# Turned first product with a copied stationary matrix, three results on the way and a load table in an adaLN block with a mixture of experts

## The chip, the cores and the metric

The kernel runs on one core of one Trainium2 chip. The metric is the device time of one execution in microseconds. PE is TensorE (its weight loads stand as PEld), DVE is VectorE, ACT is ScalarE, POOL is GpSimd, SP is SyncE, which issues most of the DMAs. A q behind an engine's name (POOLq, SPq) is its sequencer, which runs register and semaphore instructions itself.

## The reference

An input x of 16 positions x 256 rows x 256 features becomes a diffusion and reaction term, which then goes through one transformer block with a mixture of experts. Cut to what matters:

```python
x_in = diffuse(x, zX, zY, zR)                       # 16 x 256 rows of 256 features
attn = causal_attention(layernorm(x_in) @ in_proj)  # 16 heads over the 16 positions
x1   = x_in + attn @ out_proj
hn2  = layernorm(x1).reshape(4096, 256)
gates = top-2 of softmax(hn2 @ router_w.T)          # 8 experts
hmid = gelu(hn2 @ w1[e])                            # 256 -> 512, for each chosen expert e
y    = (hmid * gate) @ w2[e]                        # 512 -> 256
out  = x + x1 + y                                   # y summed over the two experts of a row
```

## The kernel before, in words

**Two halves.** A loop over `g` (32 groups of 128 rows, with a few steps ahead and behind) does diffusion, norms, attention and routing: DVE multiplies and sums the attention, PE projects and turns. Rows that are routed are scattered by POOL into a buffer in DRAM, sorted by expert (`scatter`, two indirect DMAs for each group). After each of seven sets of groups DVE makes a table of tiles of 128 rows of one expert (`route_tiles`): 71 tiles in all, with the expert in `tab`, the buffer row in `tabr`, and a count in `tabw`.

**A tile's steps.** SP loads a tile (`tile_in`). PE turns it (`turn_in`, L1062, into `b_x`), ACT applies the norm's weights while it copies it to `xT` (L565). PE multiplies by the first matrix (`up`, L1071): `xT` is the stationary operand, the expert's 512 columns of `w1_s`, addressed by a register, are the moving one, and the result `b_h` is 128 rows x 512. ACT applies the Gelu (L590) into `hm`; PE turns `hm` with four transposes (`turn_h`, L1078) into `b_t`, ACT copies that to `hmT` (L594), and PE multiplies by the second matrix (`down`, L1086, into `b_y`). ACT (L604, tiles below 47) or DVE (L764, tiles from 47 on) scales the result into one of five buffers `y`. POOL adds it to the output in DRAM with an indirect DMA that accumulates (`add_y`, L492).

**The order of the tiles.** A list written out by hand (`SLOTS`) places 39 first steps of tiles inside the loop; the other tiles follow behind the attention, one slot for each tile (`LEFT`). A slot (a, b, c, d) turns tile a in, multiplies tile b up, tile c down, and gives tile d out. In the first slot of `LEFT` a is 39 and d is 36.

**The order of the adds.** Two tiles of different experts may hold the same row, and then the second add must not start before the first has landed. Up to tile 36 POOL simply waits for the add before. From tile 37 on, `add_y` reads a threshold from the table `tabw` into a register (L485): it is one step lower where the tile's rows follow those of the tile before in the same expert's part of the buffer. POOL then waits for the semaphore against that register; a tiny instruction on `passed` (L487, "the check" below) carries the wait. Whatever the table says, at most two adds are on the way, with a semaphore for each parity. Adds 38 to 42 alternate with the scatters of the last five groups (L457).

```python
if j > IN_LOOP:
    behind = pool.value_load(tabw[0:1, j:j + 1], min_val=16, max_val=16 * ALL)
    pool.wait_ge(y_added[(j - 1) % 2], behind)
    pool.tensor_tensor(passed[:, j - IN_LOOP:j - IN_LOOP + 1], power[:, 0:1], power[:, 0:1], ALU.add)
elif j >= 1:
    pool.wait_ge(*added_to(j - 1))
if j >= 2:
    pool.wait_ge(*added_to(j - 2))
```

**The bulk loads.** SP loads w1 (eight loads of 512 KB, at g = 1 to 8), w2 (eight, at g = 3 to 10) and three of the four copies of x to the output (1 MB each, at g = 1, 3, 5) between the loads of the loop.

Of the kernel before, what the change touches and what calls it, by code (L numbers as in the profile page):

```python
# [5 lines left out]
P = 128  # L6
# [11 lines left out]
def adaln_moe_block(nc, x, zX, zY, zR, ln1_w, ln1_b, in_w, in_b, out_w, out_b, ln2_w, ln2_b,  # L18
# [25 lines left out]
    CAP = G * P + 2 * P  # L44
    ROW = H + 1 + E
    RING = 10
    NX = 4
    NY = 5
    NM = 12
# [7 lines left out]
    with ctx:  # L57
# [9 lines left out]
        def pair(name):  # L67
# [62 lines left out]
        tab = sb("tab", [P, ALL], I32)  # L130
        iota_i = tab[:, 0:TMAX + 3 * E + 1]
        tabr = sb("tabr", [P, ALL], I32)
        tabw_1 = sb("tabw_1", [P, 2 * (ALL // 2 + 1)], I32)
        tabw = tabw_1[:, 1:ALL + 1]
        passed = sb("passed", [P, 44])
        apart = tt[:, 1, 0:(TMAX + E - 1) // E, :].rearrange("p a b -> p (a b)").bitcast(I32)
        live = sb("live", [P, TMAX])

# [14 lines left out]
            sums_ready scaled du_ready stats1 stats2 rstd xhat1 xhat2 hT_ready hT_sb h2T_ready h2T_sb  # L153
            qkv_ready qk_sb v_sb sc_ready exp_ready pv_piece pv_used aT_sb o_ready x1_ready lg_ready lg_sb
            rt_sub rt_exp rt_m rt_cum rt_cum_sb slots_ready tab_ready pre_ready
            x_tr xT_sb h_ready gelu_done hT2_ready hmT_sb y_ready y_sb pre_done
            dve_chain pool_chain""".split()
        s = {n: sem(n) for n in names}
        x_in, y_added = pair("x_in"), pair("y_added")
        x1_added = [sem(f"x1_added{i}") for i in range(4)]  # L160
        xin_in = [sem(f"xin_in{i}") for i in range(NX)]
        scattered = [sem(f"scattered{i}") for i in range(NG)]
# [59 lines left out]
        for g in range(G + 3):  # L222
            for n in PLACES[WANT[g]]:
                step = next_slot((g, n))
                SLOTS[g, n].append(step)
                turned, raised, lowered, given = [i + (j is not None) for i, j in zip((turned, raised, lowered, given), step)]
        IN_LOOP = given
        while given < ALL:
            step = next_slot((G + 3, 0))
            LEFT.append(step)  # L230
            turned, raised, lowered, given = [i + (j is not None) for i, j in zip((turned, raised, lowered, given), step)]
# [8 lines left out]
        COUNT_FIRST = 10  # L240
        BY_DVE = FEW
        IDLE_UNTIL = min(g for g, n in SLOTS if any(b is not None for a, b, c, d in SLOTS[g, n]))
        W1_FROM = 1
        W2_FROM = 3

        def runs(g0, n):

# [10 lines left out]

        def added_to(j):

            return y_added[j % 2], 16 * (j // 2 + 1)

        def half_of(g):
            return ORDER[g]
# [13 lines left out]
        def _(sp):  # L278
# [44 lines left out]
            sp.wait_ge(s["bias_split"], 2)  # L323
            sp.dma_start(bias[1:2, :].bitcast(F32), blo.bitcast(F32)).then_inc(s["bias_lo_in"], 16)

            def tile_in(j):

                if j in FIRST:
                    r = group_of(j)
                    sp.wait_ge(s["tab_ready"], r + 1)  # L330
                    sp.wait_ge(scattered[r], 32 * len(GROUPS[r]))
                if j == TAIL:
                    sp.wait_ge(s["pre_done"], 16 * E)
                if j >= NX:
                    sp.wait_ge(s["x_tr"], j - NX + 1)
                if j >= NM:
                    sp.wait_ge(*added_to(j - NM))
                row = sp.value_load(tabr[0:1, j:j + 1], min_val=0, max_val=E * CAP - P)
# [11 lines left out]
            for g in range(-AHEAD, G + 3):  # L350
                if 3 <= g + AHEAD + 1 < G:
                    load(g + AHEAD + 1)
                if 0 <= g - W1_FROM < E:
                    e = g - W1_FROM
                    sp.dma_start(w1_s[:, e * HC * F:(e + 1) * HC * F].rearrange("p (k f) -> p k f", k=HC),
                                 w1[e].rearrange("(k p) f -> p k f", p=P)).then_inc(s["w1_in"], 16)
                if 0 <= g - W2_FROM < E:
                    e = g - W2_FROM
                    sp.dma_start(w2_s[:, e * FC * H:(e + 1) * FC * H].rearrange("p (k h) -> p k h", k=FC),
                                 w2[e].rearrange("(k p) h -> p k h", p=P)).then_inc(s["w2_in"], 16)  # L360
                if g % 2 and 1 <= (g + 1) // 2 < NCOPY:
                    copy_x((g + 1) // 2)
# [11 lines left out]
            for j in (ALL - 2, ALL - 1):  # L374
                sp.wait_ge(*added_to(j))

        @block.gpsimd
        def _(pool):
# [18 lines left out]
            def later_constants():  # L397
                link(pool.memset(ones_b[:, :], 1.0))

                pool.affine_select(out=lower[:, :], in_=ones_b[:, :], compare_op=ALU.is_gt, fill=0.0, base=0,  # L400
                                   pattern=[[1, P]], channel_multiplier=-1).then_inc(s["const_ready"], 1)
                pool.memset(ones_r[:, :].bitcast(F32), 1.0).then_inc(s["const_ready"], 1)
                links_of = [pool.iota(iota_i[:, 0:TMAX], [[1, TMAX]], base=0, channel_multiplier=0),
                            pool.iota(iota_i[:, TMAX:TMAX + E], [[CAP, E]], base=P, channel_multiplier=0),
                            pool.iota(iota_i[:, TMAX + E:TMAX + 2 * E], [[CAP, E]], base=P - 1, channel_multiplier=-1),
                            pool.iota(iota_i[:, TMAX + 2 * E:TMAX + 3 * E], [[P, E]], base=E * CAP, channel_multiplier=1),
                            pool.iota(iota_i[:, TMAX + 3 * E:TMAX + 3 * E + 1], [[1, 1]], base=0, channel_multiplier=1),
                            *[pool.iota(idt[:, g:g + n], [[B, n]], base=p * B + c * P, channel_multiplier=1)
                              for g, c, p, n in ((0, 0, 0, FEW), (FEW, 1, 0, FEW), (2 * FEW, 0, FEW, S - FEW), (AGAIN, 1, FEW, S - FEW))]]
                links_of.append(pool.iota(tabw_1[:, :].rearrange("p (a b) -> p a b", b=2), [[16, ALL // 2 + 1], [0, 2]],  # L410
                                          base=0, channel_multiplier=0))
                link(links_of[-1])
                pool.tensor_copy(iota_f[:, :], iota_i[:, :]).then_inc(s["const_ready"], 1)
# [64 lines left out]
            def add_y(j):  # L478

                pool.wait_ge(s["y_sb"], j + 1)  # L480
                if j in FIRST:
                    for i in range(4):
                        pool.wait_ge(x1_added[i], 16 * len([g for g in range(ENDS[group_of(j)]) if g % 4 == i]))
                if j > IN_LOOP:
                    behind = pool.value_load(tabw[0:1, j:j + 1], min_val=16, max_val=16 * ALL)  # L485
                    pool.wait_ge(y_added[(j - 1) % 2], behind)
                    pool.tensor_tensor(passed[:, j - IN_LOOP:j - IN_LOOP + 1], power[:, 0:1], power[:, 0:1], ALU.add)  # L487
                elif j >= 1:
                    pool.wait_ge(*added_to(j - 1))
                if j >= 2:  # L490
                    pool.wait_ge(*added_to(j - 2))
                pool.indirect_dma_start(out_rows, bass.IndirectOffsetOnAxis(ap=tags[:, j % NM, 0:1].bitcast(U32), axis=0),  # L492
                                        y[:, j % NY, :], None, compute_op=ALU.add).then_inc(y_added[j % 2], 16)

            def scatter_at(g, n):
                for step in SCATTER.get((g, n), ()):
# [34 lines left out]
        def _(act):  # L531
# [55 lines left out]

            def gelu(j):
                act.wait_ge(s["h_ready"], j + 1)
                act.activation(hm[:, :], b_h[:, :], ACT.Gelu).then_inc(s["gelu_done"], 1)  # L590

            def turned_h(j):
                act.wait_ge(s["hT2_ready"], j + 1)
# [11 lines left out]
                               scale=tags[:, j % NM, bass.ds(e + 1, 1)]).then_inc(s["y_sb"], 1)  # L605

            def slot(a, b, c, d):
                if c is not None:
                    turned_h(c)
                if d is not None and d < TAIL:  # L610
                    result(d)
# [85 lines left out]
                    place(g, n)  # L697
            slot(*LEFT[0])
            odds(NG - 1)
            for a, b, c, d in LEFT[1:]:  # L700
                slot(a, b, c, d)

        @block.vector
        def _(dve):
# [144 lines left out]
            def route_tiles(r):  # L849
# [43 lines left out]
                else:  # L893
# [4 lines left out]
                    need(step)  # L898
                    step = tick(dve.tensor_scalar(apart[:, 0:m], apart[:, 0:m], P, -16, ALU.is_equal, ALU.mult))
                    need(step)  # L900
                    dve.tensor_tensor(tabw[:, a:b], apart[:, 0:m], tabw[:, a:b], ALU.add).then_inc(s["tab_ready"], 1)

            for g in range(-AHEAD, G + 3):
                T = ORDER[g][1] + 1 if 0 <= g < G else 0
# [137 lines left out]
        def _(pe):  # L1042
# [32 lines left out]
            def turn_h(j):  # L1075
# [2 lines left out]
                    mm = pe.transpose(b_t[:, k * P:(k + 1) * P], hm[:, k * P:(k + 1) * P], ident[:, :])  # L1078
                mm.then_inc(s["hT2_ready"], 1)

            def down(j, e):
                pe.wait_ge(s["hmT_sb"], j + 1)
                if j >= 1:
                    pe.wait_ge(s["y_sb"], j)
                for k in range(FC):
# [9 lines left out]
            loaded = {}  # L1095

            def slot(a, b, c):
                if a == 0:
                    pe.wait_ge(s["w1_in"], 16 * E)
                    pe.wait_ge(s["w2_in"], 16 * E)  # L1100
                if b is not None:
                    loaded[b] = next_expert(b)
                if c is not None:
                    turn_h(c)
                if b is not None:
                    up(b, loaded[b])
                if a is not None:
# [174 lines left out]
```

## Time and profile before

| | |
|---|---|
| median of 3 runs | 658.73 us (656.2 to 659.06) |
| profiled execution, own time | 656.47 us |
| its span in the trace | 654.4 us |
| outside the span | 2.07 us |
| mean granted clock of TensorE | 0.955 |
| PE busy | 591.0 us (90%) |
| DVE, ACT, POOL busy | 437.4 us, 375.5 us, 428.5 us |

Matmuls are pipelined and their ends are modelled, so a matmul's own duration is longer than the distance from one to the next; where a pace matters it is read from starts. A tile's steps are spread over the engines, so the stage behind the attention (from about 507 us on) is read by the distance of the same step from tile to tile.

### The profile page before, as it was taken

To read this page: it belongs to the slowest core of one execution; us is meant where nothing else is said; L and a number is where in the kernel's file an instruction comes from. 1 tells how busy PE (TensorE), PEld (TensorE's weight loads), DVE (VectorE), ACT (ScalarE), POOL (GpSimd) and SP (SyncE) were. 2 spreads that over 40 slices of the span, in tenths; PEclk is the share of its full clock that TensorE was granted. 3 is DMA by queue.
4 is the path that set the end of the run, shared out by engine and by line. 5 is a ranking of instruction groups with operands and counts; after the bars stand their busy time and mean duration, and the time that the engine had idled before them with its cause. 6 is when DMAs were issued, how large, how long until landed. Compare 5 with 4: busy or idle time off the path is not lost.

```text
span 654.4 us, 10903 instructions
## 1 busy us (share of the span) xinstructions
PE 591.0 (90%) x2842; PEld 420.0 (64%) x2842; DVE 437.4 (67%) x1012; ACT 375.5 (57%) x860; POOL 428.5 (65%) x516
## 2 busy tenths in 40 slices
PE   6599988788969989999999999999698999999991
PEld 6356656566746757766666777777475666666661
DVE  4576899779996999999977999969950500111110
ACT  2443553357646776768887876665355655444440
POOL 4576785865894488597898788834784774444442
PEclk9887998879889999999999999999998999999997
DMA  7386662441342224334344333532344545444422
GB/s 204 100 303 187 200 195 72 116 91 49 75 99 50 58 74 83 74 59 81 83 107 76 73 67 66 108 50 43 82 78 57 103 87 90 67 66 67 67 33 24
DMA packets 61775, 59.89 MB, mean 92 GB/s; under 512 B 17610, under 2 KB 57299, under 8 KB 61652
## 3 DMA queue, kind: packets, MB, share of 16 engines
q0 software_dynamic: 18288, 23.28, 21.9%
q1 hardware_dynamic: 43428, 35.91, 19.5%
q8 instruction: 26, 0.43, 0.3%
q14 instruction: 33, 0.27, 0.1%
HBM read 35.89 MB, written 27.46 MB: 97 GB/s over the span
## 4 chain that ended last, share of the span: by engine, by line
PE 51%; DVE 19%; POOL 12%; issue 6%; ACT 5%; DMA 4%; SPq 1%; POOLq 0%; ACTq 0%; DVEq 0%
PE b_h L1071 13%; PE b_y L1086 13%; PE b_at L1251 5%; DVE qk_prod L938 5%; PE b_qk L1189 4%; DVE sc L946 4%; POOL xs_d L457 3%; PE b_t L1078 3%; PE b_at L1179 3%; DVE pv_prod L1015 3%; DMA out_dram<-y,tags 2%; PE b_v L1189 2%; POOL out_dram L492 2%; PE b_x L1062 2%; POOL dev L443 1%
## 5 line engine op out<-in xcount | busy, mean ns | idle before, releaser
L492 POOL DMA_INDIRECT out_dram<-y,tags x71 | 124.2, 1750 | 30.1 <-issue 24.3
L1086 PE MATMUL b_y<-w_s,hm_hmT 128*128 x568 | 135.2, 381 | 4.9 <-ACT y L604 3.3
L1071 PE MATMUL b_h<-w_s,xT 128*128 x284 | 134.7, 597 | 0.3
L1086 PEld LDWEIGHTS b_y<-w_s,hm_hmT 128*128 128x128 f32 x568 | 102.4, 190 | 19.2 <-issue 8.2
L938 DVE TENSOR_TENSOR qk_prod<-q,kv 128x1024 f32<-128x1024 f32 (+2 forms) x80 | 91.3, 1165 | 2.4 <-ACT kv L630 1.4
L1015 DVE TENSOR_TENSOR pv_prod<-kv,pr 128x1024 f32<-128x1024 f32 (+2 forms) x80 | 85.5, 1113 | 6.8 <-PE b_at L1251 5.6
L764 DVE TENSOR_SCALAR y<-b_y,tags,live 128x256 f32<-128x256 f32 x24 | 13.0, 544 | 113.0 <-PE b_y L1086 113.0
L1251 PE MATMUL b_at<-ident,pv_prod 128*128 128x128 f32 x544 | 72.4, 288 | 13.2 <-DVE pv_prod L1015 13.1
L457 POOL DMA_INDIRECT xs_d<-ring,slot_row x64 | 70.7, 1105 | 18.9 <-issue 18.1
L946 DVE TENSOR_REDUCE sc<-qk_prod 128x64 f32<-128x1024 f32 (+2 forms) x80 | 82.1, 1051 | 0.3
L1251 PEld LDWEIGHTS b_at<-ident,pv_prod 128*128 128x128 f32 x544 | 65.1, 149 | 18.3 <-issue 15.2
L1071 PEld LDWEIGHTS b_h<-w_s,xT 128*128 128x128 f32 x284 | 48.9, 192 | 35.3 <-issue 35.1
L590 ACT ACTIVATE hm_hmT<-b_h 128x512 f32<-128x512 f32 x71 | 42.5, 598 | 45.6 <-PE b_h L1071 45.6
L1189 PE MATMUL b_qk<-wqkv,hT 128*128 128x512 f32 x128 | 67.2, 650 | 0.3 <-ACT hT L565 0.3
L594 ACT ACTIVATE hm_hmT<-b_t 128x512 f32<-128x512 f32 x71 | 42.6, 600 | 36.0 <-PE b_t L1078 36.0
L565 ACT ACTIVATE xT<-b_x,ln 128x128 f32<-128x128 f32 x142 | 57.0, 458 | 3.6 <-PE b_x L1062 3.6
L442 POOL TENSOR_SCALAR dev<-mv 128x2 f32<-128x2 f32 (+1 forms) x37 | 14.8, 401 | 65.6 <-DVE mv L995 56.5
L1062 PEld LDWEIGHTS b_x<-ident,xin 128*128 128x128 f32 x142 | 19.8, 141 | 41.3 <-issue 39.1
L487 POOL TENSOR_TENSOR passed<-power 128x1 f32<-128x1 f32 x34 | 7.4, 218 | 58.6 <-DMA out_dram<-y,tags 54.6
L1078 PE MATMUL b_t<-ident,hm_hmT 128*128 128x128 f32 x284 | 43.4, 276 | 0.3 <-ACT hm_hmT L590 0.2
L629 ACT ACTIVATE q<-b_qk 128x256 f32<-128x256 f32 x32 | 12.0, 376 | 51.3 <-PE b_v L1189 51.3
L430 POOL TENSOR_TENSOR du<-du,xp 128x256 f32<-128x256 f32 x28 | 27.5, 981 | 20.1 <-ACT xud L545 19.9
(186 smaller groups left out, 1085.2 us busy)
## 6 DMA issues: line engine op xcount, KB each, us to landing
xin<-xs_d SPq DMA_DIRECT2D x71, 128.0 KB, 2.1
w_s<-in_L_ffn_w_dram SPq DMA_DIRECT2D x16, 512.0 KB, 4.5
xp<-in_x_dram SPq DMA_DIRECT2D x32, 128.0 KB
xud<-in_x_dram SPq DMA_DIRECT2D x32, 128.0 KB
out_dram<-x POOLq DMA_DIRECT2D x32, 128.0 KB, 3.2
xud<-in_x_dram SPq DMA_DIRECT2D x32, 126.0 KB
tags<-xs_d SPq DMA_DIRECT2D x71, 4.5 KB, 2.0
out_dram<-y,tags POOLq DMA_INDIRECT x71, 3.9
```

Of the source, the lines that this page charges most:

```text
L457: pool.indirect_dma_start(xs_d, bass.IndirectOffsetOnAxis(ap=slot_row[:, k, g:g + 1], axis=0), ring[:, g % RING, :], None).then_inc(scatte ...
L492: pool.indirect_dma_start(out_rows, bass.IndirectOffsetOnAxis(ap=tags[:, j % NM, 0:1].bitcast(U32), axis=0), y[:, j % NY, :], None, comput ...
L565: ins = act.activation(dst[:, c * P:(c + 1) * P], bank[:, c * P:(c + 1) * P], ACT.Identity, scale=ln[:, 2 * k, c:c + 1], bias=ln[:, 2 * k ...
L594: act.activation(hmT[:, :], b_t[:, :], ACT.Copy).then_inc(s["hmT_sb"], 1)
L938: made.append(tick(dve.tensor_tensor(qk_prod[:, m % 2, 0:(t1 - t0) * H].rearrange("p (t h) -> p t h", h=H), q[:, g % 2, :].rearrange("p (o ...
L946: summed.append(tick(dve.tensor_reduce(scv.rearrange("p n t -> p t n")[:, t0:t1, :], qk_prod[:, m % 2, 0:(t1 - t0) * H].rearrange("p (t n ...
L1015: dve.tensor_tensor(pv_prod[:, at % NPV, 0:(t1 - t0) * H].rearrange("p (t n d) -> p t n d", n=NH, d=D), kv[:, values_at(v, t0):values_at(v ...
L1071: mm = pe.matmul(b_h[:, :], xT[:, k * P:(k + 1) * P], w1_s[:, bass.ds(e * (HC * F) + k * F, F)], start=(k == 0), stop=(k == HC - 1))
L1078: mm = pe.transpose(b_t[:, k * P:(k + 1) * P], hm[:, k * P:(k + 1) * P], ident[:, :])
L1086: mm = pe.matmul(b_y[:, 0:H], hmT[:, k * P:(k + 1) * P], w2_s[:, bass.ds(e * (FC * H) + k * H, H)], start=(k == 0), stop=(k == FC - 1))
L1189: mm = pe.matmul(bank[:, 0:b - a], hT[:, k, :], wqkv[:, k, a:b], start=False, stop=(k == HC - 1))
L1251: mm = pe.matmul(b_at[:, k * P:(k + 1) * P], pv_prod[:, at % NPV, lo:lo + P], ident[:, :], start=(m == 0 and t == 0 and k == 0), stop=(m = ...
```

## The change

From tile 39 on (`TURNED`), the first product comes out turned: the matrix w1 of the tile's expert is the stationary operand and `xT` the moving one, so that no transposes and no copy of them follow. The stationary operand needs a fixed place, so ACT reads the tile's expert from the table and copies the 1024 columns of the matrix into one of five buffers that the attention's products have left free (`matrix`, two tiles ahead). `b_h` and `b_t` alternate as the product's bank. Three adds may be on the way in place of two (`NA`): there are two tables of thresholds, and `add_y` reads and waits for both, one behind the other. The bulk loads follow a table (`BULK`), and PE waits for w1 before the first `up` and for w2 before the first `down`.

```diff
+    NA = 3
...
-        tabw_1 = sb("tabw_1", [P, 2 * (ALL // 2 + 1)], I32)
-        tabw = tabw_1[:, 1:ALL + 1]
-        passed = sb("passed", [P, 44])
+        behind_all = sb("behind_all", [P, NA - 1, NA * (ALL // NA + 2)], I32)
+        behind = [behind_all[:, k, NA - 1 - k:NA - 1 - k + ALL] for k in range(NA - 1)]
+        passed = sb("passed", [P, (NA - 1) * 44])
...
-        W1_FROM = 1
-        W2_FROM = 3
+        BULK = {0: ("a0",), 1: ("a1",), 2: ("a2",), 3: ("a3",), 4: ("a4",), 5: ("a5",), 6: ("a6", "x1"), 7: ("a7", "b0"),
+                8: ("b1", "b2"), 9: ("b3", "b4"), 10: ("b5", "b6"), 11: ("b7", "x2"), 13: ("x3",)}
...
+        w1_bufs = [qk_prod[:, 0, :], qk_prod[:, 1, :]] + [pv_prod[:, i, :] for i in range(NPV)]
+        NW = len(w1_bufs)
+        def w1_buf(j):
+            return w1_bufs[(j - TURNED) % NW]
+        def hidden(j):
+            return ((b_h, hm), (b_t, hmT))[(j - TURNED) % 2]
...
                 if j > IN_LOOP:
-                    behind = pool.value_load(tabw[0:1, j:j + 1], min_val=16, max_val=16 * ALL)
-                    pool.wait_ge(y_added[(j - 1) % 2], behind)
-                    pool.tensor_tensor(passed[:, j - IN_LOOP:j - IN_LOOP + 1], power[:, 0:1], power[:, 0:1], ALU.add)
+                    for k in range(1, NA):
+                        least = pool.value_load(behind[k - 1][0:1, j:j + 1], min_val=16, max_val=16 * ALL)
+                        pool.wait_ge(y_added[(j - k) % NA], least)
+                        at = (NA - 1) * (j - IN_LOOP) - k
+                        pool.tensor_tensor(passed[:, at:at + 1], power[:, 0:1], power[:, 0:1], ALU.add)
                 elif j >= 1:
                     pool.wait_ge(*added_to(j - 1))
-                if j >= 2:
-                    pool.wait_ge(*added_to(j - 2))
+                if j >= NA:
+                    pool.wait_ge(*added_to(j - NA))
...
+            def matrix(j):
+                if j == TURNED:
+                    act.wait_ge(s["sc_ready"], G)
+                    act.wait_ge(s["pv_used"], PIECES[G])
+                if j in FIRST:
+                    act.wait_ge(s["tab_ready"], group_of(j) + 1)
+                e = act.value_load(tab[0:1, j:j + 1], min_val=0, max_val=E - 1)
+                if j - TURNED >= NW:
+                    act.wait_ge(s["h_ready"], j - NW + 1)
+                act.activation(w1_buf(j), w1_s[:, bass.ds(e * (HC * F), HC * F)], ACT.Copy).then_inc(s["w1_made"], 1)
...
             odds(NG - 1)
+            for j in (TURNED, TURNED + 1):
+                matrix(j)
             for a, b, c, d in LEFT[1:]:
                 slot(a, b, c, d)
+                if a is not None and a + 1 < ALL:
+                    matrix(a + 1)
...
-                    dve.tensor_tensor(tabw[:, a:b], apart[:, 0:m], tabw[:, a:b], ALU.add).then_inc(s["tab_ready"], 1)
+                    for k in range(NA - 1):
+                        ins = dve.tensor_tensor(behind[k][:, a:b], apart[:, 0:m], behind[k][:, a:b], ALU.add)
+                    ins.then_inc(s["tab_ready"], 1)
...
+            def up_turned(j):
+                bank, _ = hidden(j)
+                pe.wait_ge(s["w1_made"], j - TURNED + 1)
+                pe.wait_ge(s["xT_sb"], j + 1)
+                pe.wait_ge(s["gelu_done"], j - 1)
+                if j == TURNED + 1:
+                    pe.wait_ge(s["hmT_sb"], TURNED)
+                w = w1_buf(j).rearrange("p (k f) -> p k f", k=HC)
+                for i in range(FC):
+                    for k in range(HC):
+                        mm = pe.matmul(bank[:, i * P:(i + 1) * P], w[:, k, i * P:(i + 1) * P], xT[:, k * P:(k + 1) * P],
+                                       start=(k == 0), stop=(k == HC - 1))
+                mm.then_inc(s["h_ready"], 1)
...
-                if a == 0:
+                if b == 0:
                     pe.wait_ge(s["w1_in"], 16 * E)
+                if c == 0:
                     pe.wait_ge(s["w2_in"], 16 * E)
```

## Rows read from the trace of the kernel before

**Rows 1.** Chain that ended last, one tile's steps: start, length in us, engine and line
```profile
553.21 1.72 PE b_h L1071 x4
554.93 0.22 PE b_x L1062 x2
555.14 1.73 PE b_y L1086 x8
556.87 0.44 PE b_t L1078 x4
557.31 1.72 PE b_h L1071 x4
```

**Rows 2.** The same chain at its end, 623 us on
```profile
623.26 0.34 POOLq L485
...
623.92 0.19 POOL passed L487
624.12 0.46 issue
...
632.85 3.70 DMA out_dram<-y,tags
636.55 0.07 issue
636.62 0.19 POOL passed L487
```

**Rows 3.** POOL's waits, 538 to 650 us: total us, times, longest
```profile
POOL passed L487 <- DMA out_dram<-y,tags: 50.6, 21, 3.0
POOL passed L487 <- DVE y L764: 3.8, 4, 1.4
```

**Rows 4.** POOL's timeline: start, length, instruction, idle before and its releaser
```profile
510.71 1.54 POOL L492 DMA_INDIRECT out_dram<-y,tags  x1 [0.68 <-issue]
...
528.97 1.61 POOL L492 DMA_INDIRECT out_dram<-y,tags  x1 [0.16 <-issue]
...
533.53 1.62 POOL L492 DMA_INDIRECT out_dram<-y,tags  x1 [0.17 <-issue]
...
537.84 1.58 POOL L492 DMA_INDIRECT out_dram<-y,tags  x1 [0.22 <-ACT y L604]
...
539.80 1.57 POOL L492 DMA_INDIRECT out_dram<-y,tags  x1 [0.16 <-issue]
...
645.09 0.19 POOL L487 TENSOR_TENSOR passed<-power 128x1 f32<-128x1 f32 x1 [2.33 <-DMA out_dram<-y,tags]
645.43 1.57 POOL L492 DMA_INDIRECT out_dram<-y,tags  x1 [0.15 <-issue]
```

**Rows 5.** Lines L57 (block's end), L485 (ns min/median/max, starts), L492 (538 to 650)
```profile
L57 POOLq DRAIN  x1: 9095/9095/9095, 645.0 to 645.0; - x1
...
L485 POOLq TENSOR_LOAD <-tabw x34: 283/292/632, 509.0 to 642.6; - x34
...
DMA to landing us min/median/max: 3.7/3.9/4.5
```

**Rows 6.** ACT's timeline as the attention ends, and line L572
```profile
507.68 0.24 ACT L639 ACTIVATE odd<-odd 128x40 f32<-128x40 f32 x1
507.82 0.58 ACT L594 ACTIVATE hm_hmT<-b_t 128x512 f32<-128x512 f32 x1
...
L572 ACT ACTIVATE bias<-kv x1: 1056/1056/1056, 6.9 to 6.9; 1x1024 fp32r<-1x1024 f32 x1
```

**Rows 7.** ACT's timeline over one tile
```profile
563.17 0.60 ACT L590 ACTIVATE hm_hmT<-b_h 128x512 f32<-128x512 f32 x1 [1.12 <-PE b_h L1071]
```

**Rows 8.** Chain that ended last: 32 turns of the attention's products
```profile
483.71 3.56 PE b_at L1251 x32
```

**Rows 9.** Stages: us, busy us (count) of PE, PEld, DVE, ACT, POOL, clock, DMA share, GB/s
```profile
45.00:130.00 85.00, 74.05 (x380) 53.94 (x378) 69.72 (x188) 38.33 (x112) 63.29 (x87) 0.92 0.55 168
...
507.00:640.00 133.00, 132.21 (x588) 91.29 (x585) 20.72 (x67) 67.22 (x140) 67.46 (x75) 1.00 0.45 72
```

More of the change, by code:

```diff
@@ L155, in adaln_moe_block @@
             rt_sub rt_exp rt_m rt_cum rt_cum_sb slots_ready tab_ready pre_ready
-            x_tr xT_sb h_ready gelu_done hT2_ready hmT_sb y_ready y_sb pre_done
+            x_tr xT_sb h_ready gelu_done hT2_ready hmT_sb w1_made y_ready y_sb pre_done
             dve_chain pool_chain""".split()
         s = {n: sem(n) for n in names}
-        x_in, y_added = pair("x_in"), pair("y_added")
+        x_in = pair("x_in")
+        y_added = [sem(f"y_added{i}") for i in range(NA)]
         x1_added = [sem(f"x1_added{i}") for i in range(4)]
@@ L227, in adaln_moe_block @@
         IN_LOOP = given
+        TURNED = turned
         while given < ALL:
@@ L259, in added_to @@
         def added_to(j):
-            return y_added[j % 2], 16 * (j // 2 + 1)
+            return y_added[j % NA], 16 * (j // NA + 1)
+        w1_bufs = [qk_prod[:, 0, :], qk_prod[:, 1, :]] + [pv_prod[:, i, :] for i in range(NPV)]
[4 more added lines that the diff above has]
+            return ((b_h, hm), (b_t, hmT))[(j - TURNED) % 2]
         def half_of(g):
@@ L324, in _, with bulk @@
             sp.dma_start(bias[1:2, :].bitcast(F32), blo.bitcast(F32)).then_inc(s["bias_lo_in"], 16)
+            def bulk(what, i):
+                if what == "a":
+                    sp.dma_start(w1_s[:, i * HC * F:(i + 1) * HC * F].rearrange("p (k f) -> p k f", k=HC),
+                                 w1[i].rearrange("(k p) f -> p k f", p=P)).then_inc(s["w1_in"], 16)
+                elif what == "b":
+                    sp.dma_start(w2_s[:, i * FC * H:(i + 1) * FC * H].rearrange("p (k h) -> p k h", k=FC),
+                                 w2[i].rearrange("(k p) h -> p k h", p=P)).then_inc(s["w2_in"], 16)
+                else:
+                    copy_x(i)
             def tile_in(j):
@@ L352, in _ @@
                     load(g + AHEAD + 1)
[L353 to L362, printed above, removed]
+                for what in BULK.get(g, ()):
+                    bulk(what[0], int(what[1]))
                 for n in range(NPLACES):
@@ L373, in _ @@
                 sp.wait_ge(x1_added[i], 16 * (G // 4))
-            for j in (ALL - 2, ALL - 1):
+            for j in range(ALL - NA, ALL):
                 sp.wait_ge(*added_to(j))
@@ L409, in later_constants @@
                               for g, c, p, n in ((0, 0, 0, FEW), (FEW, 1, 0, FEW), (2 * FEW, 0, FEW, S - FEW), (AGAIN, 1, FEW, S - FEW))]]
-                links_of.append(pool.iota(tabw_1[:, :].rearrange("p (a b) -> p a b", b=2), [[16, ALL // 2 + 1], [0, 2]],
+                links_of.append(pool.iota(behind_all[:, :, :].rearrange("p k (a b) -> p k a b", b=NA), [[0, NA - 1], [16, ALL // NA + 2], [0, NA]],
                                           base=0, channel_multiplier=0))
@@ L484, in add_y @@
                 if j > IN_LOOP:
-                    behind = pool.value_load(tabw[0:1, j:j + 1], min_val=16, max_val=16 * ALL)
-                    pool.wait_ge(y_added[(j - 1) % 2], behind)
-                    pool.tensor_tensor(passed[:, j - IN_LOOP:j - IN_LOOP + 1], power[:, 0:1], power[:, 0:1], ALU.add)
+                    for k in range(1, NA):
[3 more added lines that the diff above has]
+                        pool.tensor_tensor(passed[:, at:at + 1], power[:, 0:1], power[:, 0:1], ALU.add)
                 elif j >= 1:
                     pool.wait_ge(*added_to(j - 1))
-                if j >= 2:
-                    pool.wait_ge(*added_to(j - 2))
+                if j >= NA:
+                    pool.wait_ge(*added_to(j - NA))
                 pool.indirect_dma_start(out_rows, bass.IndirectOffsetOnAxis(ap=tags[:, j % NM, 0:1].bitcast(U32), axis=0),
-                                        y[:, j % NY, :], None, compute_op=ALU.add).then_inc(y_added[j % 2], 16)
+                                        y[:, j % NY, :], None, compute_op=ALU.add).then_inc(y_added[j % NA], 16)
             def scatter_at(g, n):
@@ L589, in gelu @@
                 act.wait_ge(s["h_ready"], j + 1)
-                act.activation(hm[:, :], b_h[:, :], ACT.Gelu).then_inc(s["gelu_done"], 1)
+                if j < TURNED:
+                    act.activation(hm[:, :], b_h[:, :], ACT.Gelu).then_inc(s["gelu_done"], 1)
+                else:
+                    bank, dst = hidden(j)
+                    act.wait_ge(s["y_ready"], j - 1)
+                    act.activation(dst, bank[:, :], ACT.Gelu).then_inc(s["gelu_done"], 1)
+            def matrix(j):
[8 more added lines that the diff above has]
+                act.activation(w1_buf(j), w1_s[:, bass.ds(e * (HC * F), HC * F)], ACT.Copy).then_inc(s["w1_made"], 1)
             def turned_h(j):
@@ L607, in slot @@
             def slot(a, b, c, d):
-                if c is not None:
+                if c is not None and c < TURNED:
                     turned_h(c)
@@ L1079, in turn_h @@
                 mm.then_inc(s["hT2_ready"], 1)
-            def down(j, e):
-                pe.wait_ge(s["hmT_sb"], j + 1)
+            def up_turned(j):
[11 more added lines that the diff above has]
+                mm.then_inc(s["h_ready"], 1)
+            def down(j, e):
+                hmT = hidden(j)[1] if j >= TURNED else hm_hmT[:, F:2 * F]
+                if j < TURNED:
+                    pe.wait_ge(s["hmT_sb"], j + 1)
+                else:
+                    pe.wait_ge(s["gelu_done"], j + 1)
                 if j >= 1:
@@ L1102, in slot @@
                     loaded[b] = next_expert(b)
-                if c is not None:
+                if c is not None and c < TURNED:
                     turn_h(c)
-                if b is not None:
+                if b is not None and b < TURNED:
                     up(b, loaded[b])
+                if b is not None and b >= TURNED:
+                    up_turned(b)
                 if a is not None:
```

## The prediction

> **What bounds the kernel now.** I read the stages first, then the chain that ended last, then POOL's waits. Behind the attention PE is busy without a break (132.21 of 133 us at full clock) and a tile takes 557.31 - 553.21 = 4.10 us: 1.72 up, 0.22 turning the next tile in, 1.73 down, 0.44 for four transposes [rows 1, 9]. But near 623 us the chain leaves PE and goes from add to add through the DMAs [rows 2]. In the 27 checks from add 44 to add 70 POOL waited 21 times for an add to land (50.6 us) and 4 times for a result [rows 3]. The add is therefore a second chain that runs almost as slowly as PE, so I price both.
>
> One link of it: an add's DMA lands 3.70 us after its start, the semaphore takes 0.07, the check 0.19, and the next add starts 0.15 behind it [rows 2, 4]: 4.1 us at best. The median to landing from 538 us on is 3.9 [rows 5]; with the 0.07 that is 4.0 to the next check, so I take 4.0 + 0.34 = 4.34. Two adds of which the second need not wait start 539.80 - 537.84 = 1.96 apart [rows 4]. How many must wait? Working the routing out from the inputs, 20 of the tiles 44 to 70 do not continue the rows of the tile before (the 21st wait of the row, at 628 us, coincides with a result), and 7 do. The chain before could thus do 20 x 4.34 + 7 x 1.96 = 100.5 us; the row says 645.43 - 537.84 = 107.6, PE's pace gives 27 x 4.10 = 110.7 less the lag that add 43 had. The adds have only some 7 us to spare.
>
> **TensorE's gain.** Transposes go: 0.44. The turned product has eight 128-column products, each as two passes as in L1071's four records for two: 16 passes with a new stationary matrix each. Not in the trace with these operands; the nearest row is 32 transposes with 32 new stationary matrices and 128 moving columns in 3.56 us, 0.111 each [rows 8], so 16 x 0.111 = 1.78 against 1.72. A tile becomes 1.78 + 0.22 + 1.73 = 3.73 us, 0.37 less; for 32 tiles 11.8 us of PE work. It counts only if the adds keep up.
>
> **ScalarE.** The copy of 1024 columns took 1.06 us on one partition [rows 6]; I take that for 128, since 512 columns of 128 partitions take 0.60 [rows 7] and doubling that bounds it at 1.20. ACT loses the copy of the turned hidden values (0.60, same size as rows 7) and had 1.12 us idle before each Gelu [rows 7] beside as much before the other: hidden, tile for tile. At the entry it is not: two matrices are copied between the exponentials (507.68) and the older copy of tile 38 (507.82), behind a table read of about 0.5. That puts result 37, and add 37, some 0.5 + 2 x 1.06 = 2.6 us later.
>
> **The adds: what the change adds.** Each add now reads two thresholds, and the second read stands behind the first check. From read to check is 623.92 - 623.26 = 0.66, of which the read was 0.34 against a median of 0.29, so 0.61 [rows 2, 5]. Behind a check that had just been reached by a read the add starts 0.19 + 0.46 = 0.65 later, not 0.34 [rows 2]. Does the second read run while the first check still waits? A sequencer instruction that follows a waiting check is to be seen once: the block's end, on POOLq, starts at 645.0, although the engine stood idle for 2.33 us before, and the check of the last add is released at 645.09 [rows 4, 5]. So I take it that the read waits. From release to add: about 0.58 to the second check (the read starts 0.04 ahead of the check's own start), 0.65 to the add: 1.23 in place of 0.34, 0.9 more for each add that waits. The bounds: 0.2 (the read is hidden, a check of 0.19 remains), 0.58 (the read counts, the longer way to the add does not), 1.25 (the slowest read, 0.63 [rows 5]).
>
> The Trainium skill, page "Perfetto Trace Analysis", section "GPSIMD Engine Instruction", draws it otherwise: an instruction for the engine is pushed into a wait queue, and the sequencer is then ready for the next one. By that rule the second read would run under the first wait and the sum would be 658, the first rival below; the start of the block's end [rows 5] is this trace's evidence against it.
>
> Third place on the way: it helps only where two tiles in a row need not wait, which of 27 is one place (65, 66), at most some 2 us, and waits for an add that landed long ago elsewhere. Nothing.
>
> **The sum, against the profiled execution's 656.47 us.**
> 1. Add 37 started at 510.71 [rows 4]; entry 2.6 and its second read 0.9: 514.2.
> 2. Adds 38 to 43. A round of two scatters, check and add takes 533.53 - 528.97 = 4.56 on POOL alone [rows 4], 4.78 with the second check. Two of the six follow their predecessor's rows: 2 x 4.78; four wait: 4 x (4.34 + 0.9 = 5.24). 30.5, so add 43 starts at 544.7, 6.9 later than its 537.84.
> 3. Adds 44 to 70: 20 x 5.24 + 7 x 2.16 = 119.9, 12.3 more than 107.6. PE needs 27 x 3.73 = 100.7 there; it waits for the five y buffers and its gain is lost.
> 4. From the last add's start to the end: as before.
>
> 656.5 + 6.9 + 12.3 = 675.7; I say **675**. The last scatters land a few us later, and with them tile 47's load; its result is wanted only some ten us after. The median of the runs before stands 2.3 us above the profiled execution, which is less than anything at issue.
>
> **Costed at nothing.** Bulk loads by a table: in 45 to 130 us DMAs are busy 0.55 of the time [rows 9], and the waits view of that stretch names no DMA, so neither earlier w1 nor later copies of x shorten a wait; the last w2 load moves next to the first tile's load, which has ten us before the first down. Without that cover, 2 us either way. One more DVE instruction in six table makings: below 0.3 each, up to 1.6 if DVE is on the path every time. PE's waits for the weights: met long before.
>
> **Rivals.**
> - *The second read is hidden under the first check's wait* (not slower). The extra is 0.2: add 37 +2.8; rounds 6 x 4.78 = 28.7 (+1.6); then 20 x 4.54 + 7 x 2.0 = 104.8 (-2.8). 656.5 + 2.8 + 1.6 - 2.8 = about 658, no change. It decides at an extra of 0.2 to 0.3 for each waiting add; against it stands the start of the block's end. 0.13.
> - *The adds keep up and PE's gain comes out* (faster). The entry is hidden too and a landing link stays at 4.34: 100.7 in place of 107.6, about 650. Against it: the table read is in the chain of waits itself [rows 2]. 0.06.
> - *Stationary loads do not hide behind products of 128 columns.* If load and product add up, a pass costs 0.22, the turned product 3.56 and a tile 5.51: 32 x 1.4 = 45 us more than before, about 700. Against it: the 32 turns at 0.111 [rows 8], each with a load of the same size. 0.05. The Trainium skill's page "TensorE: Matmul & The Clock Gate", section "Part 3: Packing small matmuls — row/col tiling", says that a load overlaps products in flight only where the row group differs, which is this rival; the turns of rows 8 use the full array and disagree.
> - *The adds' chain sets the end, as summed.* 0.76. With 0.58 extra: entry and rounds +5.3, then 20 x 4.92 + 7 x 2.16 = 113.5 (+5.9): 667.7. With 1.25: about 684.
>
> **Range and chances.** 657 to 684: the main case by its bounds and the upper half of the first rival; main case alone 667 to 684. Less than 0.5% (3 us, about what a measurement of this kernel can tell from no change) faster or slower comes from the first rival: 0.11; faster: the second and a little of the first, 0.08; slower 0.81.
>
> **What would show it.** Right: between the two checks of one add some 0.6 us with a table read in it and 0.65 to the add; adds that wait 5.2 us apart; PE with gaps, its tile 3.7 us where it runs free, turned products at 0.11 us a pass; ACT idle between copies; the chain that ended last made of adds from about 515 us. Wrong: second reads that end before the first check starts; adds 4.3 apart; PE without gaps to the end; or passes at 0.2 us.

## The result and the profile after

The changed kernel takes 671.64 us (median of 6 runs, 666.78 to 677.12) where the kernel before, run beside it, takes 656.38 us (6 runs, 651.08 to 659.06). The ratio is 1.0235, with a 95% interval of 1.019 to 1.0281: slower by 15.3 us. The forecast was 675. The profiled execution of the changed kernel took 673.18 us itself, with a span of 671.0.

The page first: the span, PE's busy time, PE's and its clock's slices, then the two rows of the adds (the check L506 and the add's DMA L511).

```profile
span 671.0 us, 11687 instructions
...
PE 585.6 (87%) x3098; PEld 444.1 (66%) x3098; DVE 437.3 (65%) x1018; ACT 385.8 (57%) x860; POOL 434.5 (65%) x550
...
PE   5698998698879989999999999997889969999920
...
PEclk9887977989869999999999999999889979999965
...
L511 POOL DMA_INDIRECT out_dram<-y,tags x71 | 123.5, 1739 | 37.4 <-issue 32.1
...
L506 POOL TENSOR_TENSOR passed<-power 128x1 f32<-128x1 f32 x68 | 16.8, 314 | 62.4 <-DMA out_dram<-y,tags 49.9
```

PE has less to do than before and ends earlier: in the last two slices it is busy 2 tenths and not at all. The granted clock falls to 6 and 5 tenths in these slices; in the one before both stand at 9 (full speed is 2.4 GHz, the lower level 1.2). POOL's checks stand idle 49.9 us for adds to land, 68 of them now, two for each add.

The stages, in the columns of [rows 9]:

```profile
507.00:640.00 133.00, 123.64 (x835) 114.78 (x833) 20.54 (x67) 77.29 (x140) 66.12 (x98) 0.97 0.41 68
640.00:671.00 31.00, 2.68 (x8) 1.73 (x8) 1.09 (x2) 0.00 (x0) 10.65 (x16) 0.55 0.25 29
```

In the last 31 us PE works 2.68 us and ACT not at all; what is left is POOL's adds. The whole loss arises behind add 36, the last before the entry (the stretch in which the attention ends and the first two matrices are copied): this add starts at 506.07 where it started at 506.54 before. From POOL's timelines, first the kernel before, then adds 36, 37 and 43 of the changed one:

```profile
506.54 1.54 POOL L492 DMA_INDIRECT out_dram<-y,tags  x1 [3.00 <-issue]
```

```profile
506.07 1.54 POOL L511 DMA_INDIRECT out_dram<-y,tags  x1 [2.84 <-issue]
...
512.83 1.54 POOL L511 DMA_INDIRECT out_dram<-y,tags  x1 [0.69 <-issue]
...
543.16 1.58 POOL L511 DMA_INDIRECT out_dram<-y,tags  x1 [0.82 <-issue]
```

PE's timeline over one turned tile (start, length, line, operation, tiles, count):

```profile
516.96 1.95 PE L1134 MATMUL b_h<-xT,pv_prod 128*128 128x128 f32 x16
518.75 0.38 PE L1104 MATMUL b_x<-ident,xin 128*128 128x128 f32 x2
518.96 1.89 PE L1147 MATMUL b_y<-w_s,hm_hmT 128*128 x8
520.69 1.95 PE L1134 MATMUL b_t<-xT,pv_prod 128*128 128x128 f32 x16
```

By starts, as in [rows 1]: the turned product with its 16 passes takes 518.75 - 516.96 = 1.79 us, and a tile 520.69 - 516.96 = 3.73, where it took 4.10. TensorE's part of the change does what it says.

POOL's timeline near the end, one add behind the other (L506 is a check, L511 the add's DMA):

```profile
645.57 0.19 POOL L506 TENSOR_TENSOR passed<-power 128x1 f32<-128x1 f32 x1 [2.54 <-DMA out_dram<-y,tags]
646.13 0.19 POOL L506 TENSOR_TENSOR passed<-power 128x1 f32<-128x1 f32 x1 [0.38 <-issue]
646.79 1.56 POOL L511 DMA_INDIRECT out_dram<-y,tags  x1 [0.46 <-issue]
650.67 0.19 POOL L506 TENSOR_TENSOR passed<-power 128x1 f32<-128x1 f32 x1 [2.32 <-DMA out_dram<-y,tags]
...
662.09 1.56 POOL L511 DMA_INDIRECT out_dram<-y,tags  x1 [0.46 <-issue]
```

In the kernel before an add that had waited started 0.34 us behind the start of its only check [rows 4]. Here it takes 646.79 - 645.57 = 1.22: 0.56 to the second check and 0.66 to the add. The chain that ended last shows what fills the 0.56 (start, length, what; POOLq is POOL's own sequencer):

```profile
643.03 2.50 issue
645.53 0.23 POOLq L503
...
645.85 0.15 POOLq L503
...
646.13 0.19 POOL passed L506
646.33 0.25 issue
```

L503 is the second read of a threshold. It starts at 645.53, 0.04 us before the first check, after 2.50 us in which nothing ran. It did not run under the wait. Where the first wait was met already it is otherwise; add 66, in the same view:

```profile
639.61 0.35 POOLq L503
...
640.38 0.63 POOL passed L506
```

Here the second read starts 0.77 us ahead of the first check, while POOL still works on add 65; in the seven such adds from 44 on it is 0.62 to 0.78. So it is the wait not yet met that holds the read back here, and not a busy engine.

Last, POOL's, DVE's and PE's waits from 510 to 660 us (total us, times, longest); POOL's and DVE's lines read the same from 544 to 662 us, the stretch of adds 44 to 70:

```profile
POOL passed L506 <- DMA out_dram<-y,tags: 47.7, 20, 2.7
...
DVE y L804 <- DMA out_dram<-y,tags: 21.1, 5, 4.7
...
PE b_x L1104 <- DMA tags<-xs_d: 5.1, 1, 5.1
```

From add 44 on twenty checks wait for a landing, the number that the routing gave. The second line is new: DVE waits for a free `y` buffer, which the late adds still hold.

### The profile page after: what moved, and what is told of

Its sections match the earlier page's. It is cut to its first block and busy times, and to the rows that moved or that the text cites. A ratio compares the mean times of both kernels' runs of the same rounds, so it can differ in the third digit from the quotient of the medians.

```text
span 671.0 us, 11687 instructions
## 1 busy us (share of the span) xinstructions
PE 585.6 (87%) x3098; PEld 444.1 (66%) x3098; DVE 437.3 (65%) x1018; ACT 385.8 (57%) x860; POOL 434.5 (65%) x550
## 5 line engine op out<-in xcount | busy, mean ns | idle before, releaser
L511 POOL DMA_INDIRECT out_dram<-y,tags x71 | 123.5, 1739 | 37.4 <-issue 32.1
L1147 PE MATMUL b_y<-w_s,hm_hmT 128*128 x568 | 138.0, 387 | 8.9 <-DVE y L804 4.2
L1315 PE MATMUL b_at<-ident,pv_prod 128*128 128x128 f32 x544 | 74.0, 292 | 10.5 <-DVE pv_prod L1057 10.3
L1315 PEld LDWEIGHTS b_at<-ident,pv_prod 128*128 128x128 f32 x544 | 67.0, 152 | 15.3 <-issue 12.3
L1113 PE MATMUL b_h<-w_s,xT 128*128 x156 | 75.0, 604 | 0.3
L1253 PE MATMUL b_qk<-wqkv,hT 128*128 128x512 f32 x128 | 69.7, 672 | 0.0
L506 POOL TENSOR_TENSOR passed<-power 128x1 f32<-128x1 f32 x68 | 16.8, 314 | 62.4 <-DMA out_dram<-y,tags 49.9
L1253 PEld LDWEIGHTS b_qk<-wqkv,hT 128*128 128x128 f32 x128 | 25.8, 213 | 22.5 <-issue 20.2
L1113 PEld LDWEIGHTS b_h<-w_s,xT 128*128 128x128 f32 x156 | 27.3, 194 | 20.0 <-issue 19.9
L1243 PE MATMUL b_at<-wo,aT 128*128 128x256 f32 x128 | 39.0, 430 | 0.0
L1104 PE MATMUL b_x<-ident,xin 128*128 128x128 f32 x142 | 28.0, 280 | 11.0 <-DMA tags<-xs_d 11.0
```

The source lines that it names most:

```text
L1104: mm = pe.transpose(b_x[:, k * P:(k + 1) * P], xin[:, i, k * P:(k + 1) * P], ident[:, :])
L1113: mm = pe.matmul(b_h[:, :], xT[:, k * P:(k + 1) * P], w1_s[:, bass.ds(e * (HC * F) + k * F, F)], start=(k == 0), stop=(k == HC - 1))
L1147: mm = pe.matmul(b_y[:, 0:H], hmT[:, k * P:(k + 1) * P], w2_s[:, bass.ds(e * (FC * H) + k * H, H)], start=(k == 0), stop=(k == FC - 1))
L1243: mm = pe.matmul(b_at[:, H:2 * H], aT[:, k, :], wo[:, k, :], start=False, stop=(k == HC - 1))
L1253: mm = pe.matmul(bank[:, 0:b - a], hT[:, k, :], wqkv[:, k, a:b], start=False, stop=(k == HC - 1))
L1315: mm = pe.matmul(b_at[:, k * P:(k + 1) * P], pv_prod[:, at % NPV, lo:lo + P], ident[:, :], start=(m == 0 and t == 0 and k == 0), stop=(m = ...
```

## Experiments

The theory is the prediction's: an add that waits carries a second read and a longer way to its DMA, and this chain sets the end. The rivals are another source of the loss (ScalarE's copies, the turned product, the load table) and a cause in the number of adds on the way instead of the read. One stretch settles most of it without the run-to-run shift of the attention: from the start of add 36 to the start of add 70, read from POOL's timeline of each run. Before, it is 645.43 - 506.54 = 138.9 us. The run with the load table alone, whose program behind add 36 is that of the kernel before, gives 139.8: differences of 1 us in this stretch tell nothing. The expected times were reckoned from some 656 us for the kernel before; beside the experiments it took 652.93 and 652.52, so it is the ratios that compare.

| kernel | add 36 to add 70, us | against before | ratio of medians (95%) |
|---|---|---|---|
| changed kernel | 156.0 | +17.1 | 1.0235 (1.019 to 1.0281) |
| two adds on the way | 134.95 | -3.94 | 0.9916 (0.9877 to 0.9956) |
| three adds alone | 156.7 | +17.8 | 1.0307 (1.0263 to 1.035) |
| both reads first | 141.1 | +2.2 | 1.0029 (0.9992 to 1.0065) |
| third read | 172.1 | +33.2 | one run: 689.01 us |
| two adds, earlier copies | 132.8 | -6.1 | 0.992 (0.9886 to 0.9953) |
| load table alone | 139.8 | +0.9 | 1.000 (0.9964 to 1.0036) |

**Two adds on the way.** The changed kernel with one number back:

```diff
-    NA = 3
+    NA = 2
```

> The changed kernel with two adds on the way and one threshold read for each add, as before; the turned product, the matrix copies and the load table stay. If the second read behind the first check is the cost, an add that waits costs 4.34 us again in place of 5.24; the copies at the entry still put add 37 about 1.5 us later (as the trace after shows); the 27 last adds take 100.5 to 104 us, because TensorE now delivers a tile every 3.73 us: about 651 us, faster than before. Rival, the turned product or its copies on ScalarE are the cost: near 670 us, as after. Rival, the load table is the cost: also near 670.

It took 648.11 us (10 runs, 644.64 to 652.41) beside 652.93 of the kernel before: 0.8% faster than that one (0.4 to 1.2%), and far below the changed kernel. Its POOL timeline at the end:

```profile
631.19 0.19 POOL L506 TENSOR_TENSOR passed<-power 128x1 f32<-128x1 f32 x1 [2.26 <-DMA out_dram<-y,tags]
631.53 1.56 POOL L511 DMA_INDIRECT out_dram<-y,tags  x1 [0.15 <-DVE y L804]
635.46 0.19 POOL L506 TENSOR_TENSOR passed<-power 128x1 f32<-128x1 f32 x1 [2.36 <-DMA out_dram<-y,tags]
635.79 1.57 POOL L511 DMA_INDIRECT out_dram<-y,tags  x1 [0.15 <-issue]
```

With one read and one check the way from release to add is 0.34 again, and two waiting adds stand 635.79 - 631.53 = 4.26 us apart. So ScalarE's copies, the turned product and the load table together give more than they cost.

**Three adds alone.** The kernel before with only the adds' part of the change (`NA`, two tables of thresholds, the loop of reads and checks, the DVE instruction that fills the second table):

```diff
+    NA = 3
...
-                    behind = pool.value_load(tabw[0:1, j:j + 1], min_val=16, max_val=16 * ALL)
-                    pool.wait_ge(y_added[(j - 1) % 2], behind)
+                    for k in range(1, NA):
+                        least = pool.value_load(behind[k - 1][0:1, j:j + 1], min_val=16, max_val=16 * ALL)
+                        pool.wait_ge(y_added[(j - k) % NA], least)
...
```

> The kernel before with nothing changed but the adds: three on the way, two tables of thresholds, two reads for each add. If the reads are the cost: add 37 0.9 us later, adds 38 to 43 3.4 us, the last 27 adds 119.9 us in place of 107.6, so about 673 us, slower than the whole change, which at least has results ready earlier. Rival, the turned product or the loads are the cost: 656 us, as before.

It took 670.75 us (4 runs, 667.35 to 673.76). One add of its POOL timeline:

```profile
650.40 0.19 POOL L491 TENSOR_TENSOR passed<-power 128x1 f32<-128x1 f32 x1 [2.26 <-DMA out_dram<-y,tags]
650.96 0.19 POOL L491 TENSOR_TENSOR passed<-power 128x1 f32<-128x1 f32 x1 [0.37 <-issue]
651.62 1.56 POOL L496 DMA_INDIRECT out_dram<-y,tags  x1 [0.46 <-issue]
```

The same 1.22 us from the first check to the add, and the whole loss, with no turned tile in the kernel. Whether the rest of the change gives a little back beside three adds (1.0307 against 1.0235) stays open: the two intervals overlap, and in the stretch they differ by 0.7 us.

**Both reads first.** The changed kernel, three adds on the way as in it, with the second read moved ahead of the first check:

```diff
-                    for k in range(1, NA):
-                        least = pool.value_load(behind[k - 1][0:1, j:j + 1], min_val=16, max_val=16 * ALL)
-                        pool.wait_ge(y_added[(j - k) % NA], least)
+                    least = [pool.value_load(behind[k - 1][0:1, j:j + 1], min_val=16, max_val=16 * ALL) for k in range(1, NA)]
+                    for k in range(1, NA):
+                        pool.wait_ge(y_added[(j - k) % NA], least[k - 1])
```

> The changed kernel with both thresholds of an add read before the first check; waits, checks and the three places on the way stay. If what costs is that the second read can only start when the first check is released, check 2 follows check 1 by 0.14 to 0.2 us in place of 0.57, the add follows check 2 by 0.34 in place of 0.66, an add that waits costs 4.5 us, and the time is about 657 us. Rival, a third add on the way (its DMA, its semaphore, a longer landing) is the cost: near 671 us, as after.

It took 654.21 us (10 runs, 651.46 to 659.07). Two adds of its POOL timeline; "x2" is both checks of one add:

```profile
638.20 0.33 POOL L506 TENSOR_TENSOR passed<-power 128x1 f32<-128x1 f32 x2 [2.31 <-DMA out_dram<-y,tags]
638.68 1.56 POOL L511 DMA_INDIRECT out_dram<-y,tags  x1 [0.15 <-issue]
642.61 0.34 POOL L506 TENSOR_TENSOR passed<-power 128x1 f32<-128x1 f32 x2 [2.36 <-DMA out_dram<-y,tags]
643.09 1.57 POOL L511 DMA_INDIRECT out_dram<-y,tags  x1
```

From the first check to the add it is 643.09 - 642.61 = 0.48 in place of 1.22, although the same two reads and two checks are made. The chain that ended last shows where the reads of the last add went (L502 is the line of both):

```profile
638.16 0.23 POOLq L502
...
639.22 3.34 issue
```

They run from 638.16 to 639.2, right behind the release of the add before, and are done 3.4 us before the last add's first check. Of 0.88 us that the second threshold cost (1.22 less 0.34), the place of the read made 0.74, the second check itself 0.14. This tells the place of the read from the number of adds on the way: 156.0 - 141.1 = 14.9 us of the stretch hang on one line's place. The third place itself is still no gain: beside two adds the stretch is 6.1 us longer (141.1 against 134.95), and the intervals of the two ratios don't touch. The second check accounts for some 3.8 of it (0.14 in each of the last 27 adds); the rest was not traced.

**A third read.** The changed kernel with one more read and check behind the two (the table of the second is read again, so the wait is met):

```diff
+                    least = pool.value_load(behind[1][0:1, j:j + 1], min_val=16, max_val=16 * ALL)
+                    pool.wait_ge(y_added[(j - 2) % NA], least)
+                    at = (NA - 1) * 44 + j - IN_LOOP - 1
+                    pool.tensor_tensor(passed[:, at:at + 1], power[:, 0:1], power[:, 0:1], ALU.add)
...
```

> The changed kernel with a third read and a third check in each add, which repeats the second one's wait and so holds nothing back by itself. If a read behind a released check is the price, each of the 24 adds that wait costs 0.57 us more, 14 us in all: about 685 us in this look. Rival, the reads are covered and something else bounds the adds: 672 us.

One run took 689.01 us. One add of its POOL timeline (L510 is the third check):

```profile
558.65 0.19 POOL L506 TENSOR_TENSOR passed<-power 128x1 f32<-128x1 f32 x1 [2.37 <-DMA out_dram<-y,tags]
559.21 0.19 POOL L506 TENSOR_TENSOR passed<-power 128x1 f32<-128x1 f32 x1 [0.37 <-issue]
559.80 0.20 POOL L510 TENSOR_TENSOR passed<-power 128x1 f32<-128x1 f32 x1 [0.39 <-issue]
560.46 1.57 POOL L515 DMA_INDIRECT out_dram<-y,tags  x1 [0.46 <-DVE y L808]
```

The third read and check cost another 0.59 us on the path, less than the 0.88 of the second, since the longer way to the DMA is not paid twice. The stretch grows by another 16.1 us; the step from two adds on the way to three was 156.0 - 134.95 = 21.1. So the cost grows with each read behind a check (one run).

**No order among the adds.** From tile 37 on the changed kernel writes each result into a DRAM buffer of its own, with a wait only for the DMA of three tiles earlier; the sum of these tiles into the output is left out.

```diff
+                    if j >= NA:
+                        pool.wait_ge(*added_to(j - NA))
+                    pool.dma_start(ys_d[j * P:(j + 1) * P, :], y[:, j % NY, :]).then_inc(y_added[j % NA], 16)
+                    return
...
```

> The changed kernel, in which tiles from 37 on are not added to the output but written to a buffer of their own in DRAM, without thresholds, reads and checks: no add waits for another (this leaves out the sum over the experts for these tiles). It shows what TensorE's shorter tile is worth where the adds hold nothing back. If TensorE's gain is real and was only covered by the adds, a tile takes 3.73 us throughout, result 70 comes about 126 us after result 37 (134 before), PE is busy without gaps up to the end, and the time is 640 to 647 us. Rival, the turned product or its copies hold something else back: result 70 comes 134 us or more after result 37.

One run took 637.79 us. Its window from 510 to 620 us, in the columns of [rows 9], and two of its waits there:

```profile
510.00:620.00 110.00, 110.00 (x765) 103.81 (x764) 12.22 (x27) 69.20 (x127) 23.77 (x37) 1.00 0.28 79
```

```profile
DVE y L804 <- PE b_y L1147: 94.7, 21, 30.9
POOL ys_d L505 <- DVE y L804: 66.9, 21, 3.5
```

PE is busy throughout at full clock, POOL waits for results and no longer for landings, and result 70 comes 122.0 us after result 37, where it came 133.7 after it before. So PE's gain is real, 11.7 us, and it was the adds that covered it.

**Two adds, copies earlier.** The best version so far, with the first two matrices copied one slot earlier, ahead of the Gelu of the tile before, so that they do not stand in the entry:

```diff
-    NA = 3
+    NA = 2
...
+                if a == TURNED - 1:
+                    for j in (TURNED, TURNED + 1):
+                        matrix(j)
...
-            for j in (TURNED, TURNED + 1):
-                matrix(j)
```

> Two adds on the way with one read (as in the first run), and the copies of the first two matrices moved one slot ahead, to where ScalarE waits for a product before its Gelu. If they cost 1.5 us at the entry because they stood between the exponentials and the copy of tile 38, result 37 comes that much earlier, and so does the whole chain of adds: 1 to 1.5 us under the first run, ratio to before about 0.989. Rival, the slot before has no room on ScalarE: the same as the first run or later.

It took 646.6 us (12 runs, 644.96 to 651.33). Result 37 came 4.39 us behind result 36, against 6.11 with two adds alone, so the entry's cost is gone from the trace; the ratio 0.992 (0.9886 to 0.9953) does not tell this version from the other.

**The load table alone.** The kernel before with `BULK` and the later waits for the weights, and nothing else:

```diff
-        W1_FROM = 1
-        W2_FROM = 3
+        BULK = {0: ("a0",), 1: ("a1",), 2: ("a2",), 3: ("a3",), 4: ("a4",), 5: ("a5",), 6: ("a6", "x1"), 7: ("a7", "b0"),
+                8: ("b1", "b2"), 9: ("b3", "b4"), 10: ("b5", "b6"), 11: ("b7", "x2"), 13: ("x3",)}
...
```

> The kernel before with the load table and the later waits for the weights alone. If no transfer of the loop waited for the bulk loads, the ratio to before is 1.000 within 0.3%. Rival, the table smooths the DMAs in the first 130 us: up to 2 us faster; or the copies of x behind the first tile's load delay it: up to 2 us slower.

It took 652.8 us (12 runs, 650.46 to 659.54) beside 652.52: ratio 1.000 (0.9964 to 1.0036). The table costs and gives nothing that this comparison can tell.

## Why the prediction was right

**TensorE.** Summed: 1.78 + 0.22 + 1.73 = 3.73 us a tile. Measured: 3.73, with 1.79 for the turned product, so 0.112 a pass. The rival in which stationary loads stay in view is out. The Trainium skill, "TensorE: Matmul & The Clock Gate", section "Part 3: Packing small matmuls — row/col tiling", says in its list that a load overlaps only where the row group differs; a few lines earlier it also lets a load be pulled ahead that goes to the background weight buffer, which the prediction left out. This trace shows 16 passes over the full array, each with a new stationary matrix, at the pace of [rows 8]: it is against the list and agrees with the earlier sentence. No row shows which buffer a load used.

**The add that waits.** Summed: 0.58 to the second check and 0.65 to the add, 5.24 us from add to add. Measured: 0.56 and 0.66; adds 43 to 70 take 662.09 - 543.16 = 118.9 against 119.9 forecast, which with 7 steps of 2.08 is 5.22 for each of the 20 others. The first rival, the read hidden under the wait, is refuted twice: by the start of L503 at the release, and by the run with both reads first, which should then have changed nothing. The Trainium skill, "Perfetto Trace Analysis", section "GPSIMD Engine Instruction", has the sequencer ready for the next instruction while one waits for its semaphore; this trace shows no read under a wait in any of the 20 waiting adds from 44 on, where the second read starts 0.04 us before the first check each time. The runs do not tell whether the check's wait is held by the sequencer itself, in which case that section does not speak of it.

**Adds 38 to 43.** Summed: 30.5 us. Measured: 543.16 - 512.83 = 30.3, in steps of 4.68 to 5.41. Right as a sum; but adds 39, 41 and 42 took their 5.2 us less from a landing than from POOL's own round of scatters (4.2 us to the first check) with the second read partly behind it.

**Terms that were mis-sized.** The entry was put at 2.6 us for result 37. It took 1.5. ACT's timeline there, and one copy within the tiles:

```profile
507.47 0.24 ACT L675 ACTIVATE odd<-odd 128x40 f32<-128x40 f32 x1
507.62 1.99 ACT L626 ACTIVATE qk_prod<-w_s 128x1024 f32 x2
509.51 0.58 ACT L630 ACTIVATE hm_hmT<-b_t 128x512 f32<-128x512 f32 x1
...
550.27 1.06 ACT L626 ACTIVATE qk_prod<-w_s 128x1024 f32 x1
```

The older copy of tile 38 (L630) starts 509.51 - 507.47 = 2.04 us behind the last exponential, where it started 0.14 behind it before [rows 6]: 1.9 us. The two copies took what was summed for them, 1.99 against 2.12, but the table's read of 0.5 did not count: the copies start before the exponential ends. Result 37 came 1.5 us later than before (509.98 against 508.45). The second read took 0.59 at add 37 and not 0.9, since the way from check to add was 0.87 there before already. From add 36 to add 37 it is 512.83 - 506.07 = 6.76 us, 2.6 more than the 4.17 before, where 3.5 was summed. That is 0.9 us of the 2.5 by which the sum was too long (675.7 against the profiled 673.18); adds 43 to 70 account for 1.0, and add 36 itself, 0.5 earlier than before, for the most of the rest.

**Third place on the way.** Said: it helps at one place, at most some 2 us. Adds 65 and 66 start 2.08 us apart with three. With two they start 3.64 apart in the first run and 2.14 in the one with earlier copies: between nothing and 1.6 us, at that one place.

**A cover that was thinner than said.** Tile 47's load was named as late and harmless, because its own result is wanted only some ten us later. PE waited 5.1 us for it, and in the kernel's order the turn of tile 47 stands ahead of the second product of tile 45. PE's timeline:

```profile
542.66 0.69 PE L1104 MATMUL b_x<-ident,xin 128*128 128x128 f32 x2 [5.09 <-DMA tags<-xs_d]
543.14 3.62 PE L1147 MATMUL b_y<-w_s,hm_hmT 128*128 x8
```

So it was result 45 that came late, at 547.37, 10.9 us behind result 44. It cost next to nothing because add 45 was still waiting for a landing at 549.35; the run with both reads first, whose adds come faster, shows what it can cost: there add 45 starts 545.05 - 539.11 = 5.94 us behind add 44, where most waiting adds take 4.3 to 4.6. That the slow adds covered it in the changed kernel was luck for the sum.

**A sign that did not come.** The chain that ended last was to be made of adds from about 515 us. The profile's chain has them without a break only from 604 us on; from 543 to 603 it runs through PE, which has no gap from 552 to 620 us.

```profile
603.39 0.55 DVE y L804
...
604.08 1.56 POOL out_dram L511
```

This does not make PE the bound there: counted in order, the result at 603.39 is tile 60's and the add at 604.08 is add 57, whose own result was done at 592.74. The chain seems to take the last event before the add for its release. The steps from add to add, 5.0 to 5.5 us for those that wait, run through the same stretch.

**Where the gain went.** Before, adds 43 to 70 took 107.6 us. The prediction worked out that a chain with one read could do them in 100.5; with two adds on the way and the faster tiles it did them in 635.79 - 534.00 = 101.8. So of PE's 11.7 us only 5.8 come out behind add 43, and the entry (5.95 us from add 36 to add 37 in that kernel, 4.17 before) takes 1.8 of them back, which leaves about the 3.94 of the table.

## What to carry to other kernels

Beside the engine that is busy, price the chain of ordered transfers link by link: when it runs within a few per cent of the engine, a shorter step of the engine pays only up to it, and a longer link costs at once, times the number of links. A register read that a wait needs belongs ahead of the previous wait, not behind it; its place made 14.9 us here. An extra transfer on the way is worth what the data's own order leaves for it, which is counted from the data before the code is written.

## What the runs showed of the hardware

- The add's DMA starts 0.34 us behind a check that was released from a wait, and 0.66 behind a check that follows a read made just before. With both reads first the gap is 0.34 again behind the second check (642.75 to 643.09, the second check of the pair above), so the longer way belongs to the read between the checks, not to the second check. What POOL does in these 0.3 us no row shows.
- A register read behind a check whose wait is not yet met starts 0.04 us before that check starts, in all 20 such adds from 44 on in the changed kernel; behind a check whose wait is met it starts 0.62 to 0.78 us ahead of the check, in the other seven.
- ACT copies 1024 columns over 128 partitions within SBUF in 1.06 us, the same as 1024 columns of one partition [rows 6], and two such copies in a row in 1.99.
